# Prelude sums on TensorE, early mask matrices and expert weights rounded ahead of the attention steps

## What is computed

```python
x = x + attention(layernorm(x), ctx, ctx, mask)     # 16 heads of 8
h = layernorm(x)
top2 = top_k(h @ router_w.T + router_bias, 2)       # 16 experts, 64 wide
x = x + sum over the two experts of softmax weight * (silu(h @ gate) * (h @ up)) @ down
      + (silu(h @ sh_gate.T) * (h @ sh_up.T)) @ sh_down.T
```

## Time and profile before

| | us |
|---|---|
| median of 3 runs | 188.59 (188.44 to 189.77) |
| the profiled execution | 188.98 |
| its span, first to last instruction | 187.2 |
| PE busy | 168.3 (90%) |
| DVE busy | 162.1 (87%) |
| ACT busy | 123.4 (66%) |
| POOL busy | 81.0 (43%) |

### The profile page before, as it was taken

The page is one execution under the profiler, slowest core; times in us unless marked ns, Lnnn a source line. Parts: engine busy times, 40 slices in busy tenths (PEclk is TensorE's granted clock), DMA queues, the critical chain, the costliest instruction groups (busy, mean ns, idle before and its releaser), DMA issues.

```text
span 187.2 us, 4388 instructions
## 1 busy us (share of the span) xinstructions
PE 168.3 (90%) x1512; PEld 131.6 (70%) x1512; DVE 162.1 (87%) x436; ACT 123.4 (66%) x282; POOL 81.0 (43%) x145
## 2 busy tenths in 40 slices
PE   7586798998989899889999989999999999999962
PEld 7554556665767677666777668888888878888841
DVE  6899999698989999988992998998998899889961
ACT  2293567686888888888889566475566555665531
POOL 5765993558688888797663523030000000000000
PEclk9999999999999999999999999999999999999995
DMA  5997700000000000001400222422554254614401
GB/s 135 315 242 187 298 12 4 2 4 2 4 0 4 0 5 0 4 0 59 158 23 0 60 105 73 121 102 87 138 173 124 71 139 127 157 72 142 81 0 56
DMA packets 13060, 15.37 MB, mean 82 GB/s; under 512 B 1520, under 2 KB 8048, under 8 KB 12912
## 3 DMA queue, kind: packets, MB, share of 16 engines
q1 hardware_dynamic: 12608, 14.57, 26.6%
q10 hardware_dynamic: 432, 0.55, 1.2%
HBM read 13.93 MB, written 1.18 MB: 81 GB/s over the span
## 4 chain that ended last, share of the span: by engine, by line
PE 39%; DVE 32%; ACT 10%; POOL 10%; issue 6%; DMA 2%; DVEq 0%; ACTq 0%
PE bank L1105 31%; DVE prob L804 5%; DVE smax L802 5%; PE bank L1058 4%; ACT prob L564 3%; POOL k_blk L435 3%; DVE v_all L842 3%; DVE xn L704 3%; POOL w_lo L462 2%; DVE xn L700 2%; DVE hid L880 2%; POOL rstd L469 2%; DVE stats L690 2%; DMA x_sb<-x 2%; ACT hid_hi L634 2%
## 5 line engine op out<-in xcount | busy, mean ns | idle before, releaser
L625 ACT ACTIVATE sig<-bank 128x512 f32<-128x512 f32 x36 | 21.6, 600 | 21.8 <-PE bank L1105 21.4
L1105 PE MATMUL bank<-xt_hi,w_hi 128*128 128x512 f32 (+1 forms) x72 | 29.2, 406 | 0.0
L1105 PE MATMUL bank<-xt_lo,w_hi 128*128 128x512 f32 (+1 forms) x72 | 28.4, 394 | 0.0
L1105 PE MATMUL bank<-xt_hi,w_lo 128*128 128x512 f32 (+1 forms) x72 | 28.2, 391 | 0.0
L863 DVE TENSOR_TENSOR hid_u<-sig,bank 128x512 f32<-128x512 f32 x32 | 21.9, 685 | 4.3 <-PE bank L1105 3.1
L804 DVE TENSOR_TENSOR prob<-bank,smax 128x512 f32<-128x512 f32 x32 | 22.1, 692 | 1.1
L1058 PE MATMUL bank<-k_blk,q_blk 64*128 64x256 f32 x128 | 18.1, 402 | 5.3 <-POOL k_blk L435 4.7
L559 ACT COPY prob_t<-bank 128x512 f32<-128x512 f32 x32 | 17.3, 589 | 8.3 <-PE bank L1034 8.3
L802 DVE TENSOR_REDUCE smax<-bank 128x8 f32<-128x512 f32 x32 | 21.8, 681 | 0.8 <-PE bank L1058 0.8
L564 ACT ACTIVATE prob<-prob 128x512 f32<-128x512 f32 x32 | 20.1, 628 | 1.1 <-DVE prob L804 0.7
L872 DVE TENSOR_TENSOR hid_lo<-hid,hid_hi 128x512 fp32r<-128x512 f32 x24 | 16.6, 690 | 1.3 <-ACT hid_hi L634 0.5
(11 more groups left out here) (113 smaller groups left out, 383.4 us busy)
## 6 DMA issues: line engine op xcount, KB each, us to landing
mix_all<-w_rows SPq DMA_DIRECT2D x64, 128.0 KB, 3.0
w_moe_sb<-w_moe SPq DMA_DIRECT2D x1, 1728.0 KB, 10.3
x_sb<-x SPq DMA_DIRECT2D x4, 256.0 KB, 7.1
ctxt_sb<-ctx_t SPq DMA_DIRECT2D x4, 256.0 KB, 6.0
ctx_sb<-ctx_nat SPq DMA_DIRECT2D x4, 256.0 KB, 5.1
out<-x_sb SPq DMA_DIRECT2D x3, 256.0 KB, 2.3
w_att_sb<-w_att ACTq DMA_DIRECT2D x1, 272.0 KB, 6.4
mrow<-mask_row ACTq DMA_DIRECT2D x1, 256.0 KB, 5.2
```

The source lines that it names most:

```text
L625: nc.scalar.activation(sig[r][:, :], gate_ps[r][:, :], ACT.Silu).then_inc(s_sig, 1)
L1105: last = nc.tensor.matmul(out, w, moving, start=start and k == 0, stop=stop and k == 2)
```

## The change

It consists of five edits.

1. **Identity on PE.** POOL no longer adds the identity to `mix_all`. Instead each cmix product is two products accumulated in PSUM: context times mask matrix, then context times identity.
2. **Early mask matrices.** ACT makes all four mask rows at its start instead of one per group. POOL's prelude is reordered: matrices 0 and 1 before the second 1/deviation, 2 and 3 right behind it, then the blocks of tile 0, and so on.
3. **Shares later.** The two share copies of DVE move from ahead of group 1's statistics to behind `scale1(2)`.
4. **Weights rounded early.** ACT rounds slices 0 to 5 after group 2's `k_all` copy (behind a wait for `w_moe`), slices 6 and 7 after group 3's, and slices 8 to 15 in steps 0 to 7; steps 8 to 15 hold none.
5. **Low parts outside the steps.** POOL forms low parts 0 to 5 before the steps, 6 and 7 in step 0, 8 to 10 in step 14, 11 to 13 in step 15 and 14 and 15 behind the steps; in every case after `norm2` and `k_blocks`.

```diff
@@ POOL, prelude
                 nc.gpsimd.tensor_tensor(
                     blk, blk,
                     inv_half[...]
-                    .broadcast_to([P, GT * BPT, S]), ALU.mult).then_inc(s_mean, 1)
-                pool.wait_ge(s_mean, g + 1)
-                nc.gpsimd.tensor_tensor(mix, mix, ident_sb.rearrange("p (o s) -> p o s", o=1).broadcast_to([P, GT, P]),
-                                        ALU.add).then_inc(s_mix, 1)
+                    .broadcast_to([P, GT * BPT, S]), ALU.mult).then_inc(s_mix, 1)
...
-            for g in range(GROUPS):
-                mix_of(g)
-                if g == GROUPS - 2:
-                    pool.wait_ge(s_q_sb, 1)
-                    pool.wait_ge(s_k_sb, 1)
-                    q_block(0, 0, first=True)
-                    k_blocks(0, 0)
-                if g + 1 < GROUPS:
-                    rstd1_of(g + 1)
+            mix_of(0)
+            mix_of(1)
+            rstd1_of(1)
+            mix_of(2)
+            mix_of(3)
+            rstd1_of(2)
+            pool.wait_ge(s_q_sb, 1)
+            pool.wait_ge(s_k_sb, 1)
+            q_block(0, 0, first=True)
+            k_blocks(0, 0)
+            rstd1_of(3)
             q_block(1, 1, first=True)
             k_blocks(1, 1)
-            pool.wait_ge(s_q_sb, GROUPS)
-            pool.wait_ge(s_k_sb, GROUPS)
@@ POOL, steps (FIRST_LOW = 6)
                 if on(-2):
                     q_block(t + 2, p, first=False)
-                if on(1):
-                    low_weights(t - 1)
                 if on(2):
                     norm2(t - 2, p)
                 if on(-2):
                     k_blocks(t + 2, p)
+                if t == 0:
+                    for u in range(FIRST_LOW, TILES // 2):
+                        low_weights(u)
+                elif t == TILES - 2:
+                    for u in range(TILES // 2, TILES // 2 + 3):
+                        low_weights(u)
+                elif t == TILES - 1:
+                    for u in range(TILES // 2 + 3, TILES // 2 + 6):
+                        low_weights(u)
...
             pool.wait_ge(s_wmoe, 16)
+            for u in range(FIRST_LOW):
+                low_weights(u)
+            pool.wait_ge(s_q_sb, GROUPS)
+            pool.wait_ge(s_k_sb, GROUPS)
             pipeline(pool, step)
             norm2(TILES - 2, 0)
+            low_weights(TILES - 2)
+            low_weights(TILES - 1)
             low_tokens(TILES - 4, 0)
-            low_weights(TILES - 1)
@@ ACT
             act.wait_ge(s_mask_row, 16)
-            mask_row_of(0)
+            for g in range(GROUPS):
+                mask_row_of(g)
...
                 nc.scalar.copy(k_all[...], k_ps[...]).then_inc(s_k_sb, 1)
+                if g == GROUPS - 2:
+                    act.wait_ge(s_wmoe, 16)
+                    for t in range(FIRST_LOW):
+                        high_weights(t)
+                if g == GROUPS - 1:
+                    for t in range(FIRST_LOW, TILES // 2):
+                        high_weights(t)
...
-                if t >= 0:
-                    high_weights(t)
+                if 0 <= t < TILES // 2:
+                    high_weights(t + TILES // 2)
@@ DVE, in the loop over groups
                 if g + 1 < GROUPS:
                     scale1(g + 1, 1 - p)
+                if g == 1:
+                    shares()
@@ PE, project
                 for i in range(GT):
-                    last = nc.tensor.matmul(cmix_ps[:, i * P:(i + 1) * P], ctxv_sb[p][:, i, :], mix_all[:, g * GT + i, :],
-                                            start=True, stop=True)
+                    nc.tensor.matmul(cmix_ps[:, i * P:(i + 1) * P], ctxv_sb[p][:, i, :], mix_all[:, g * GT + i, :],
+                                     start=True, stop=False)
+                    last = nc.tensor.matmul(cmix_ps[:, i * P:(i + 1) * P], ctxv_sb[p][:, i, :], ident_sb,
+                                            start=False, stop=True)
```

More of the change, by code:

```diff
@@ L156, in build_program @@
         s_mrow = sem("s_mrow")
-        s_mean = sem("s_mean")
         s_mix = sem("s_mix")
@@ L266, in build_program @@
         LEAD = -1
+        FIRST_LOW = 6
         STEPS = 4
@@ L536, in project @@
                 nc.scalar.copy(xt_sb[p][:, :], xt_ps[:, :]).then_inc(s_xt_sb, 1)
-                if g + 1 < GROUPS:
-                    mask_row_of(g + 1)
                 act.wait_ge(s_cmix, g + 1)
@@ L651, in slot @@
                     weights_to_sbuf(2)
-            act.wait_ge(s_wmoe, 16)
             for t in range(LEAD + 1, TILES - 1):
@@ L727, in _, with shares @@
             scale1(0, 0)
-            dve.wait_ge(s_share, 1)
-            for h in range(2):
-                dve.wait_ge(s_zero[h], 1)
-            for e in range(2):
-                rows = slice(e * S, (e + 1) * S)
-                nc.vector.tensor_copy(
-                    v_all[rows, :, :, :, e, DK].rearrange("p t b j -> p (t b) j"),
-                    share_key[rows, :].rearrange("p (c o) -> p c o", o=1).broadcast_to([S, BATCHES, PAIRS])).then_inc(s_vden, 1)
+            def shares():
+                dve.wait_ge(s_share, 1)
+                for h in range(2):
+                    dve.wait_ge(s_zero[h], 1)
+                for e in range(2):
+                    rows = slice(e * S, (e + 1) * S)
+                    nc.vector.tensor_copy(
+                        v_all[rows, :, :, :, e, DK].rearrange("p t b j -> p (t b) j"),
+                        share_key[rows, :].rearrange("p (c o) -> p c o", o=1).broadcast_to([S, BATCHES, PAIRS])).then_inc(s_vden, 1)
             def top_two(part):
@@ L837, in _ @@
                 dve.wait_ge(s_v, g + 1)
+                if g == 0:
+                    dve.wait_ge(s_share, 1)
+                    for h in range(2):
+                        dve.wait_ge(s_zero[h], 1)
                 for b in range(BPT):
```

## The result

The changed kernel takes **184.09 us** (median of 4 runs, 183.6 to 184.42) beside 188.51 for the kernel before on the same chip: ratio 0.976, 95% interval 0.973 to 0.978, a gain of 4.4 us (188.59, ahead of the prediction, was the median of three of the four runs of before). The forecast was 185.7 with a range from 184.5 to 187.8: faster, as it said, but by 1.6 us more than the forecast, and 0.4 outside its range. The profiled execution of the kernel after took 183.6 with a span of 181.7, and is the fastest of its four; that of before took 188.98 and 187.2, and is not.

What follows compares the result with a forecast made beforehand. Steps were bound by a chain of waits (POOL for ACT's rounding, PE for POOL, DVE for PE), the prelude by DVE. Steps -3.3, prelude +0.25, tail +0.15 sum to -2.9: from 188.59 to 185.7 us, range 184.5 to 187.8.

Steps and rivals of the forecast that it cites:

- The three rings: Steps: DVE alone 3.92, PE alone 3.94, POOL's path 4.72; a plain step takes 3.95, one without router 3.90.
- POOL's path: Steps: from DVE's aggregate end through norm2 and scores to the reciprocal, 4.72, equal to when DVE wants it.
- steps stop at 4.1: Rival, steps: ACT and PE have little room, gain only 1.2, 187.8 us; chance 0.12.
- does nothing: Rival, steps: low part only took slack, another link at 4.3 per step, gain 0, 189.0 us; chance 0.05.
- slower, the weights' landing: Rival, prelude: ACT's wait for w_moe delays xt_sb of group 3 from a landing of about 27.9; chance 0.03.
- shares are slow copies: Rival, prelude: DVE's two share copies cost 2.57 instead of 0.6 even without POOL beside them, 187.1 us; chance 0.10.
- DVE adds what hangs in single steps and is unchanged ... together 2.2.: Steps: two comparisons at 0.7 each, 0.4 for the two weights, 0.4 for gap and cast, added to 51.2.
- 3.7 if DVE alone decides: Steps: upper end of the forecast gain of 3.3, if DVE alone sets the step.
- no gain at a link of 4.3: Steps: lower end of the forecast gain, 0 if another link already sits at 4.3 per step.
- a loss of 0.25: Prelude: scores of tile 1 at about 32.4 against 32.13, PE becoming the bound; bounds -1.0 and +1.7.
- Prelude gains too: Rival, prelude: identity products hide behind the same stationary tile, scores of tile 1 about 1.0 earlier, 184.4 us; chance 0.10.
- +0.15: Tail: low parts 14 and 15 both fall where DVE is full, one extra collision; bounds 0 and 0.6.

Runs made afterwards that it cites:

- e3_order_only: Kernel before with one line moved: each step's low part behind norm2 and the k blocks, rounding still in every step; 185.62 us (0.985).
- e4_old_place: Changed kernel, roundings early, but each low part back in its old place ahead of norm2, one per step; 185.95 us (0.986).
- e1_weights_only: Kernel before with edits 4 and 5 alone (roundings early, low parts outside the steps), old prelude; 184.19 us (0.978).
- e2_prelude_only: Changed kernel with edits 4 and 5 undone, so new prelude with the old splitting of weights; 188.22 us (0.998).
- e8b_low_in_slack: Changed kernel with low parts 8 to 14 in steps 1 to 7 and 15 in step 9, behind the k blocks; 184.39 us (0.978).
- e12_x1_later: Changed kernel with one load moved: x of group 1 issued behind x of group 2; 187.86 us (0.994).

## Why the prediction was right and wrong

**What held.** The direction, the stage and the chain: POOL behind ACT's rounding, PE behind the k blocks, DVE behind the rows. The three rings gave 3.90 and 3.95 for a plain step; the kernel after has 3.90 to 3.98. A tie was forecast for POOL's path, and PE's waits for the k blocks are down to 0.5 us in all. The weights land at 25.2 (issued at 15.36, 9.8 on the way), 2.7 before the landing at which the forecast put the first delay. The rivals "steps stop at 4.1", "does nothing" and "slower, the weights' landing" fell with that. The copies take 0.42 each with POOL idle, nearer to the 0.3 of the forecast than to the 1.3 of its rival "shares are slow copies". By the Trainium skill, "SBUF — State Buffer", section "Who interferes with whom", a copy of DVE can be in a mode that uses the pair of ports that it shares with GpSimd, and then whichever of the two issues first holds the pair for its whole instruction. The runs agree, with 2.57, 1.67 and 0.83 for one pair of copies beside two operations of POOL, the rest of one, and none.

**The step that failed, in the steps.** "DVE adds what hangs in single steps and is unchanged ... together 2.2." It is 52.52 - 51.2 = 1.3, so the steps gained 4.2 and not 3.3. The two comparisons were taken at 0.7 each from the earlier trace rows, the row of 0.65 at 70.25 among them. That row is not the price of a comparison. It is a comparison beside a POOL q block, in the kernel before:

```profile
70.21 0.61 POOL L428 TENSOR_TENSOR q_blk<-q_all,consts_sb 128x256 f32<-128x256 f32 x1
...
70.82 0.21 DVE L744 TENSOR_TENSOR comb_b<-consts_sb,top_f 128x64 f32<-128x64 f32 x1
```

Where no q block runs, a comparison takes 0.21, and 0.30 where only the last 0.2 of one stands beside it (66.89, above). When POOL moves in the step, such a collision moves or goes; here the pair, up to the residual behind it, fell from 0.71 and 0.69 (70.25 to 70.96, 88.09 to 88.78) to 0.36 and 0.35 (66.89 to 67.25, 83.40 to 83.75). This is 0.7 of the 0.9 that the term was too large by. e3_order_only and e4_old_place show the other side: with POOL's queue only a little different the two steps with a comparison take 4.93 and 5.47, or 4.95 and 5.37, instead of 4.47 twice. The bound "3.7 if DVE alone decides" was taken with the same 2.2 and was therefore no bound; and its other end, no gain at a link of 4.3, should read 4.2 ((56.68 - 2.2) / 13). The forecast used this very rule for the share copies and did not ask it of a row of 0.65 beside a sister row of 0.21 in the steps.

**The step that failed, in the prelude.** The forecast was a loss of 0.25: group 1 starts 0.6 earlier (x "lands at about 9.7"), and from there PE takes 22.6 to the scores of tile 1 instead of 21.73. The profiled execution had 1.01 earlier (9.39), and 21.87. Of the 0.73 between 22.6 and 21.87, 0.24 lie on DVE's side, from the statistics to the transposes of group 1 (15.76 - 9.8 in the forecast, 15.11 - 9.39 in the profile). The rest is pitch, the time from the start of one of PE's operations to the next: a group was put at 5.37 and takes 5.18 (24.53 - 19.35). An added product costs 0.225 and not 0.245, the values 0.99 and not 1.05, and the transposes 0.44 where PE doesn't come out of a wait (20.34 to 20.78) and not the 0.49 of the earlier trace rows that did. The sum of the two, -0.87, is of one execution. The landing of x of group 1 scatters, from 9.05 to 11.11 in the executions in which DVE waits for it and the loads are issued in the old order, and the copies no longer cover it; in the old prelude DVE starts group 1 at 10.40 to 10.61, behind the copies. The median of the experiment with the prelude alone, -0.3, is what the edits are worth, their part of the tail included.

**The rival that came nearest.** "Prelude gains too" named 184.4, and the measurement is 184.09, but its mechanism is not what happened: the identity products are not hidden behind a stationary tile, they cost 0.90 per group and 1.01 of the prelude. The forecast's mechanism was right for 3.3 of the 4.2 in the steps, and the rest came from the collision term.

**The tail.** +0.15 was forecast for the last two low parts. Against the old places of the low parts next to nothing shows: 82.96 beside 82.97 (e1_weights_only, before), 83.29 beside 83.22 (after, e2_prelude_only). Without any late low part the tail is 0.19 shorter (e8b_low_in_slack), and one collision is there as expected: `gap`, 0.15 us in the steps, takes 0.39 beside the two low parts that POOL starts at 99.47. But all kernels with the new prelude have 83.07 to 83.30, those with the old one 82.81 to 82.97. These 0.1 to 0.3 us go with the edits 1 to 3 (0.25 from before to e2_prelude_only), although no instruction of theirs lies in the tail. The first place where the timelines part is an operation of DVE (`L883`) 8.9 us behind the residual of step 15; in the kernel after it starts 0.23 later than in e1_weights_only, with no wait shown. Why is left open.

Together on the median: steps -4.2, edits 1 to 3 with their part of the tail -0.3, late low parts 0 to +0.1, sum -4.4 to -4.5, against the -4.4 measured, whose interval is half a microsecond to either side. The forecast had -3.3, +0.25 and +0.15.

## What to carry to other kernels

Before an operation's duration goes into a sum as its price, look for a sister row of the same shape that is shorter. If there is one, look what the other engines do beside the long row: here it was a collision each time, and a change that moves the other engine's queue moves it too, for better or worse. Moving a low-priority operation behind the one that others wait for gave two thirds of this gain with one line; what was missing lay in collisions with DVE's small router operations, and so depended on the steps that the low parts were in. And when work that covered a load is moved away, the start of the work can follow the landing of that load, as the eight profiles here show: forecast a spread there and judge by a median, not by one profile.

## What the runs showed of the hardware

- A small operation of DVE started beside a longer one of POOL ended with it, within 0.1 us: a comparison of 128x64 took 0.65 instead of 0.21, a cast of 128x8 0.66 instead of 0.17, two operations of 128x4 0.85 instead of 0.32, each beside a q block of 0.61. In each the loss is what was left of POOL's operation, whatever the size of DVE's.
- PE's granted clock fell to 0.50 (1.2 GHz) after stretches in which it was busy 1.32 of 4 us (e12_x1_later; back at 1.00 in the stretch from 26 us on, PE having been busy throughout from 20 us on) and at the end of some executions, where one kernel had 1.00 in one execution and 0.58 in the other from 176 to 178 us. In that execution of e12_x1_later 3.65 us of delay by a load made the scores 6.3 us late. Half the clock need not cost anything: e1_weights_only was granted 0.57 from 16 to 20 us, its mask products of group 1 took 1.91 instead of 1.06, and still its distance is 21.75, as with the other kernels of the old prelude, in which PE waits for DVE there.
- Twelve loads issued within the first 8 us (nine by SP, three by ACT) land with a scatter: x of group 1 (256 KB) was there between 9.05 and 11.11, with the same kernel at 9.39 and at 9.05.
